# Output projection and FFN one slot later, in the order Q, O, V, F, K, in a fused linear-attention and FFN kernel

## The reference, cut to what matters

```python
q, k, v = x @ Wq.T + bq, x @ Wk.T + bk, x @ Wv.T + bv      # each cut into 16 heads of 32
q, k = exp(q), exp(k)
kv  = cumsum(k[:, :, :, None] * v[:, :, None, :], axis=1)  # running sums over the 2048 rows
k1  = cumsum(k, axis=1)
num = einsum('zsD,zsDd->zsd', q, kv)
den = sum(q * k1, axis=-1, keepdims=True)
x1  = layernorm(x + (num / den as 512 columns) @ Wo.T + bo)
h   = x1 @ weight @ aux_weight1 @ aux_weight2
out = layernorm(x1 + tanh(h + bias))
```

## Time and profile before

| | |
|---|---|
| median of 3 runs | 2304.31 us (2303.34 to 2304.90) |
| the profiled execution | 2303.22 us, of which the span of its records is 2301.4 us |
| granted clock of PE over the span | 0.993 |
| busy share of the span | PE 97%, PE weight loads 80%, DVE 70%, POOL 56%, ACT 44% |
| DMA | 243.17 MB moved, 106 GB/s on average |

### The profile page before, as it was taken

How to read it: one execution, slowest core, us unless ns; L and a number is a source line. 1 busy time by engine, 2 the same in 40 slices (tenths; PEclk the granted TensorE clock), 3 DMA queues, 4 the chain that set the end, 5 groups by cost and what they waited for, 6 DMA issues and landing times.

```text
span 2301.4 us, 77308 instructions
## 1 busy us (share of the span) xinstructions
PE 2241.9 (97%) x27752; PEld 1829.6 (80%) x27752; DVE 1617.2 (70%) x2456; ACT 1012.3 (44%) x1695; POOL 1294.2 (56%) x1797
## 2 busy tenths in 40 slices
PE   7999999999999999999999999999999999999985
PEld 6778888888888888888888888888888888887864
DVE  5576776776776776776776776776776776767674
ACT  4344444444444444444444444444444444444432
POOL 1356556556556556556556555555555555555554
PEclk9999999999999999999999999999999999999997
DMA  7133333333333333333333333333333333333221
GB/s 183 57 110 111 104 111 111 103 111 112 103 110 112 103 111 111 102 111 112 102 109 114 103 110 112 103 111 111 104 112 109 105 108 112 106 103 108 71 70 56
DMA packets 294574, 243.17 MB, mean 106 GB/s; under 512 B 33424, under 2 KB 225936, under 8 KB 294288
## 3 DMA queue, kind: packets, MB, share of 16 engines
q1 hardware_dynamic: 293136, 236.59, 33.3%
q10 hardware_dynamic: 1152, 2.10, 0.3%
HBM read 139.99 MB, written 98.57 MB: 104 GB/s over the span
## 4 chain that ended last, share of the span: by engine, by line
PE 95%; DVE 2%; issue 1%; SPq 1%; ACT 1%; DMA 1%; POOL 0%; POOLq 0%; DVEq 0%; ACTq 0%
PE SC L326 26%; PE SC L328 25%; PE SC L327 25%; PE SC L417 6%; PE ND L393 5%; PE ND L384 3%; PE ND L380 2%; PE ND L428 2%; DVE o L803 1%; DMA WK<-wT 0%; SPq L253 0%; ACT A L648 0%; DVE WK L816 0%; SPq L241 0%; PE ND L327 0%
## 5 line engine op out<-in xcount | busy, mean ns | idle before, releaser
L916 POOL TENSOR_SCALAR_AFFINE_SELECT A<-A 128x512 f32<-128x512 f32 x512 | 331.8, 682 | 321.1 <-ACT A L648 321.0
L803 DVE RECIPROCAL o<-ND 128x512 f32<-128x512 f32 x128 | 427.8, 3342 | 0.1
L857 DVE TENSOR_TENSOR xres<-SC,xres 128x512 f32<-128x512 f32 x128 | 88.5, 692 | 431.8 <-PE SC L328 431.6
L910 POOL TENSOR_TENSOR oL<-o,oH 128x512 fp32r<-128x512 f32 x128 | 166.4, 1300 | 327.0 <-ACT oH L627 327.0
L638 ACT ACTIVATE WK<-xres,shift,rstd 128x512 f32<-128x512 f32 x128 | 104.1, 814 | 531.7 <-POOL shift L951 531.7
L648 ACT ACTIVATE A<-SC 128x512 f32<-128x512 f32 x512 | 264.7, 603 | 43.3 <-PE SC L417 43.3
L326 PE MATMUL SC<-xTH,WqH 128*128 128x512 f32 x512 | 210.8, 412 | 9.5 <-ACT QT L598 3.7
L326 PE MATMUL SC<-WfH,x1H 128*128 128x512 f32 x512 | 201.0, 393 | 14.4 <-issue 7.9
L816 DVE TENSOR_TENSOR_SCAN WK<-ones,k,KT 128x128 f32<-128x128 f32 x512 | 207.5, 467 | 7.1 <-PE ND L380 6.8
L326 PE MATMUL SC<-WoH,oH 128*128 128x512 f32 x512 | 201.1, 393 | 11.3 <-issue 9.3
L598 ACT ACTIVATE QT<-SC,bcol 128x512 f32<-128x512 f32 x128 | 88.4, 690 | 270.4 <-PE SC L328 270.4
(11 more groups left out here) (103 smaller groups left out, 4983.3 us busy)
## 6 DMA issues: line engine op xcount, KB each, us to landing
xres<-x SPq DMA_DIRECT2D x128, 256.0 KB, 2.6
x_rows<-WK SPq DMA_DIRECT2D x128, 256.0 KB, 3.1
WK<-x_rows SPq DMA_DIRECT2D x512, 64.0 KB, 2.0
out<-WK SPq DMA_DIRECT2D x128, 256.0 KB, 2.0
xin<-x SPq DMA_DIRECT2D x504, 64.0 KB, 1.9
k_rows<-WK SPq DMA_DIRECT2D x120, 256.0 KB, 2.0
WK<-k_rows SPq DMA_DIRECT2D x480, 64.0 KB, 2.2
A<-a1T ACTq DMA_DIRECT2D x4, 256.0 KB, 5.4
```

Of the source, the lines that this page charges most:

```text
L803: nc.vector.reciprocal(o[:, :, :], den_ps).then_inc(recip_ready, 1)
L857: nc.vector.tensor_tensor(r, oproj_ps, r, ALU.add).then_inc(r_ready, 1)
L910: nc.gpsimd.tensor_tensor(oL[:, :, :], o[:, :, :], oH[:, :, :].bitcast(F32), ALU.subtract).then_inc(ol_ready, 1)
L916: last = nc.gpsimd.affine_select(out=A[:, k % 2, j, :, :], in_=A[:, k % 2, j, :, :], compare_op=ALU.is_ge, fill=0.0, base=0, pattern=[[0, ...
```

## The change

The tail of O and F moves by one slot: in slot k, O is that of tile k-2 and F that of tile k-3; the program has one more slot at its end (`run_slots(..., 4)`). PE's slot is now `first_half` (small, Q, O, V) and `second_half` (F, K), and K is the last product ahead of the next slot's scores. The other engines' slots are written in a new order to match. DVE turns x1s of tile k-3 ahead of the reciprocal of tile k-1, and z is the last instruction of its slot. ACT makes x1 after the copy of V and takes K's exponential late; POOL makes `x1L` ahead of `oL`; SP stores and loads K, loads x, and only then stores x1 and loads it back.

The block loads are written in another form: each of the four transfers fills all 128 partitions with one piece, and on the DRAM side it is 4 groups by 32 rows by one piece (`x_b`, `k_blocks`, `x1_blocks`, `load_blocks`). At the start of the program the loads of the two auxiliary weights go from ACT's queue to SP's, between those of x, and the loads of Wq and Wk go from SP's queue to ACT's; the splitting of the FFN weight (`split_w`) stands behind the first exponential of K.

```diff
-    x_b = x.rearrange("b (i t p) (a f) -> b i a p t f", t=P // HD, p=HD, a=HG)
+    x_b = x.rearrange("b (i t p) (a f) -> b i t a p f", t=P // HD, p=HD, a=HG)
...
-    k_blocks = k_rows.rearrange("(a p) (t c) -> t p a c", a=HG, t=HG)
-    x1_blocks = x1_rows.rearrange("(t p) (a f) -> a p t f", t=HG, a=HG)
+    k_blocks = k_rows.rearrange("(a p) (t c) -> a t p c", a=HG, t=HG)
+    x1_blocks = x1_rows.rearrange("(t p) (a f) -> t a p f", t=HG, a=HG)
...
+        def load_blocks(engine, tile, a, semaphore):
+
+            rows = a.rearrange("(a f p) n -> f a p n", a=HG, p=HD)
+            for f in range(NK):
+                engine.dma_start(tile[:, f, :], rows[f]).then_inc(semaphore, 16)
...
-            def load_by_block(tile, a, semaphore):
-                rows = a.rearrange("(a f p) n -> a p f n", a=HG, p=HD)
-                for j in range(HG):
-                    sp.dma_start(tile[j * HD:(j + 1) * HD], rows[j]).then_inc(semaphore, 16)
...
             def load_x(c, n):
-                for j in range(HG):
-                    sp.dma_start(x_buffer(c, n)[j * HD:(j + 1) * HD, :].rearrange("p (t f) -> p t f", t=HG),
-                                 x_b[n % B, c.it + n // B, j]).then_inc(xin_loaded[n % B], 16)
+                for t in range(HG):
+                    sp.dma_start(x_buffer(c, n)[:, t * P:(t + 1) * P],
+                                 x_b[n % B, c.it + n // B, t]).then_inc(xin_loaded[n % B], 16)
...
+                    for a in range(HG):
+                        sp.dma_start(Ktok[:, a * P:(a + 1) * P], k_blocks[a]).then_inc(ktok_loaded[n % B], 16)
...
                     wait_before(sp, (x1_stored[n % B], c.dma_count(n)), (x1l_ready, c.count(n)))
-                    for j in range(HG):
-                        sp.dma_start(x1s[j * HD:(j + 1) * HD, :].rearrange("p (t f) -> p t f", t=HG),
-                                     x1_blocks[j]).then_inc(x1s_loaded[n % B], 16)
...
+                    for t in range(HG):
+                        sp.dma_start(x1s[:, t * P:(t + 1) * P], x1_blocks[t]).then_inc(x1s_loaded[n % B], 16)
...
             first = Chunk(0)
+            load_aux(0)
             load_x(first, 0)
+            load_aux(1)
             load_x(first, 1)
-            load_by_block(wq_raw, wqT, wq_loaded)
+            load_aux(2)
             load_x(first, 2)
+            load_aux(3)
             load_x(first, 3)
-            load_by_block(wk_raw, wkT, wk_loaded)
             load_biases()
...
-                    wait(pe, z_ready, c.count(k - 2))
+                    wait(pe, z_ready, c.count(k - 3))
                     wait(pe, k_ready, c.count(k + 4))
                     wait(pe, v_ready, c.count(k))
-                    wait(pe, r_ready, c.count(k - 1))
+                    wait(pe, r_ready, c.count(k - 2))
...
+            def first_half(c, k):
+                small(c, k)
+                if c.exists(k + 4):
+                    queries(c, k)
+                    if c.exists(k - 2):
+                        output_projection(c, k)
+                if c.exists(k):
+                    values(c, k)
+                    if not c.exists(k + 1):
+                        denominators(c, k)
+                        attend(c, k)
+
+            def second_half(c, k):
+                if c.exists(k - 2) and not c.exists(k + 4):
+                    output_projection(c, k)
+                if c.exists(k - 3):
+                    feed_forward(c, k)
+                if c.exists(k + 4):
+                    keys(c, k)
...
             split_aux(0)
+            load_blocks(act, wq_raw, wqT, wq_loaded)
             split_aux(1)
+            load_blocks(act, wk_raw, wkT, wk_loaded)
...
             split_wq_wk(0)
             split_wq_wk(1)
-            split_w()
             split_a12()
...
-            keep_q(*ahead(-4))
-            split_x(*ahead(-4))
-            keep_k(*ahead(-4))
+            keep_q(*place(-4))
+            split_x(*place(-4))
+            keep_k(*place(-4))
+            split_w()
...
+                if c.exists(k - 3):
+                    n = k - 3
+                    wait(dve, x1s_loaded[n % B], c.part_count(n))
+                    nc.vector.transpose(x1s[:, :], x1s[:, :]).then_inc(x1_turned, 1)
+                if att and c.exists(k - 1):
                     normalise(k - 1)
```

More of the change, by code:

```diff
@@ L217, in updates_state, with place @@
                 return not self.static() or 0 <= B * self.it + n < NT - B
-        def ahead(tile):
+        def place(tile):
             return Chunk(tile // B), tile % B
@@ new lines, in _, with align, keys @@
+            f_place, k_place = 0, 48
+            def align(c, place):
+                if not c.static():
+                    pe.addr_align(256, offset=place, max_nops=255)
+            def keys(c, k):
+                align(c, k_place)
+                b, ns, att = k % QUAD, 1 - (k // QUAD) % 2, c.exists(k)
+                if not att:
+                    pe.wait_ge(wkh_ready, b + 1)
+                    pe.wait_ge(wkl_ready, b + 1)
+                if att:
+                    wait(pe, scores_out[1], c.count(k + 1))
+                wait(pe, k_ready, c.count(k + 4))
+                three_pass(kproj_ps, lambda f: WkH[:, f, b * P:(b + 1) * P],
+                           lambda f: WkL[:, f, b * P:(b + 1) * P], lambda f: xTH[:, ns, f, :],
+                           lambda f: xTL[:, ns, f, :], None if c.static() else k_place).then_inc(kproj_done, 1)
@@ L521, in _ @@
             multiply_aux()
-            queries_and_keys(*ahead(-4))
-            queries_and_keys(*ahead(-3))
+            queries(*place(-4))
+            keys(*place(-4))
+            queries(*place(-3))
+            keys(*place(-3))
             multiply_weight()
-            queries_and_keys(*ahead(-2))
-            queries_and_keys(*ahead(-1))
+            queries(*place(-2))
+            keys(*place(-2))
+            queries(*place(-1))
+            keys(*place(-1))
             multiply_bv()
@@ L538, in _ @@
                 for k in range(B):
[L539 to L547 removed]
+                    second_half(c, k)
+                    first_half(c, k + 1)
+            second_half(*place(NT - 2 * B))
+            for t in range(NT - 2 * B + 1, NT + 3):
+                first_half(*place(t))
+                second_half(*place(t))
         @block.scalar
@@ L672, in slot, with copy_v @@
                                          scale=rstd[:, 1:2]).then_inc(out_ready, 1)
-                if att and not c.exists(k + 1):
-                    split_o(k)
-            def aux_rows(a, f):
-                return a.rearrange("(k p) n -> k p n", p=P)[f]
-            for f in range(NK):
-                act.dma_start(a1T_raw[:, f, :], aux_rows(a1T, f)).then_inc(aux_loaded[f], 16)
-                act.dma_start(a2_raw[:, f, :], aux_rows(a2, f)).then_inc(aux_loaded[f], 16)
+            def copy_v(c, k):
+                wait(act, v_done, c.count(k + 1))
+                wait(act, state_done, c.state_count(k - 1))
+                nc.scalar.activation(V[:, k % 2, :], v_ps, ACT.Copy).then_inc(v_ready, 1)
             split_aux(0)
+            load_blocks(act, wq_raw, wqT, wq_loaded)
             split_aux(1)
-            split_x(*ahead(-8))
+            load_blocks(act, wk_raw, wkT, wk_loaded)
+            split_x(*place(-8))
             split_aux(2)
-            split_x(*ahead(-7))
+            split_x(*place(-7))
             split_aux(3)
-            split_x(*ahead(-6))
-            split_x(*ahead(-5))
+            split_x(*place(-6))
+            split_x(*place(-5))
             split_wq_wk(0)
             split_wq_wk(1)
-            split_w()
             split_a12()
@@ L846, in slot @@
+                if att and c.exists(k - 1):
+                    normalise(k - 1)
+                if att and not c.exists(k + 1):
+                    normalise(k)
                 if c.exists(k - 2):
                     n = k - 2
-                    wait(dve, x1s_loaded[n % B], c.part_count(n))
-                    nc.vector.transpose(x1s[:, :], x1s[:, :]).then_inc(x1_turned, 1)
-                if att and not c.exists(k + 1):
-                    normalise(k)
-                if prev:
-                    wait(dve, xres_loaded[(k - 1) % B], c.dma_count(k - 1))
+                    wait(dve, xres_loaded[n % B], c.dma_count(n))
@@ L863, in _ @@
+                if c.exists(k - 3):
+                    n = k - 3
+                    wait(dve, ffn_done, c.count(n + 1))
+                    wait(dve, out_stored[(n - 2) % B], c.dma_count(n - 2))
+                    nc.vector.tensor_tensor(y[:, n % 2, :], ffn_ps, bfbc[:, :], ALU.add).then_inc(z_ready, 1)
             first = Chunk(0)
@@ L886, in _ @@
             add_bo()
-            run_slots(dve, slot, 3)
+            run_slots(dve, slot, 4)
         @block.gpsimd
```

366 lines of the change are left out of this document (155 added, 211 removed).

## The result

The changed kernel takes 2395.6 us (2390.8 to 2399.0) against 2304.5: 1.0395 times as long, with a 95% interval of 1.0376 to 1.0413, or +91 us. The forecast was slower, +62.5, 2367 us in a range of 2299 to 2460.

A forecast was written before the change was run, and what follows sets the result against it. The prediction took PE's own stream to bound the loop. Its terms, 18.5 - 3 + 20 + 11 + 8 + 8 = +62.5 us, on a median of 2304.3 gave 2367 us, in a range of 2299 to 2460.

The forecast's parts named there:

- the forecast's own case: Whole kernel: four engines carry the block loads and the slot just fits; 2367 us, chance 0.42, own range 2345 to 2395.
- Four engines or 16: Block loads: whether their new form confines each transfer to four DMA engines, as forecast, or leaves it on all 16.
- The start, +20: Up to slot 3: loads on four engines bring slot 0's Q at 97 us, not 68.39; +20 net of smaller gains.
- K's wait, +18.5: Ahead of the scores: K's exponential, first in the list of waits, comes late; 0.15 us a slot, 121 slots, +18.5.
- The circle, +11: In the loop: turn of x1s, reciprocal, x1, store, loads, next turn; 16.8 to 17.3 us against 17.4, just fitting, +11.
- The rival in which the circle becomes the slot's bound: In the loop: the four engines, or the circle through them, set the slot; +67 instead of 11, 2423 us, chance 0.30.
- The loop's exit, -3: Where the loop is left: one slot more of slack for O and F covers the late input to PE; -3 us.
- Last slots and drain, +8 and +8: After slot 124: one more round of O, x1 and F, less waits for oL, +8; five rounds 1.7 longer each, +8.
- The rival of 16 engines: Whole kernel: all 16 engines carry the loads, K's wait is paid, the start gains 14; 2314 us, chance 0.17.
- the gain of 5.6 from the late split: At the start: splitting the FFN weight later removes PE's idle 3.74; with auxiliary weights and Wq from two queues, 5.6.

The follow-up runs named there:

- e1: The changed kernel with all block loads (x, x1s, Ktok, four weights) written wide, as before the change: 2331.1 us, 1.0112 times before.
- e2: The kernel before with nothing but its block loads in the changed, narrow form: 2344.3 us, 1.017 times before.
- e5: e1 with the scores' wait for K's exponential moved from first to last in their list, which has one entry fewer: 2315.5 us, 1.0052 times before.
- e6: e1 with the products of F and K exchanged, so that F is last again: 2314.0 us, 1.0047 times before.
- e8: The kernel before with the scores reordered and the wait for F's sum put on the first matmul into bank 0: 2309.8 us, 1.0024 times before.
- e3: The changed kernel, narrow loads kept, with the turn of x1s put behind the reciprocal and multiplication on DVE: 2369.0 us, 1.0274 times before.
- e4: The changed kernel with only the x1s loads in the wide form of before: 2364.4 us, 1.0255 times before.
- e9: The changed kernel with e1, e3 and e6 combined, the start's load order of before, and O ahead of F in the drain: 2296.0 us, 0.9967 times before.
- e7: The changed kernel with the diffs of e1 and e3 together: wide loads and the late turn of x1s: 2325.1 us, 1.0087 times before.
- e10: The kernel before with only the split of the FFN weight moved behind the first exponentials of Q and K: 2301.0 us, 0.9986 times before.

## Why the prediction was right or wrong

The direction, the cause and the range held; the size was 62.5 where 91 came (95.9 between the two profiled spans), and 2395.6 lies just above the 2345 to 2395 that I gave the forecast's own case. Term by term:

- *Four engines or 16.* Right, by the count of completion packets and by e1 and e2. By the Trainium skill ("DMA: Bandwidth & Descriptors", "Why a DMA increments its semaphore by 16 and not by 1") the number of engines is the largest one up to 16 that divides the slowest dimension of both sides, which is four for 128 and 4. The trace agrees: 12 completion packets fewer for each of 1520 transfers. The "plain division" in my words had no row behind it.
- *The start, +20.* Measured +24.2, with Q of slot 0 at 100.9 for my 97, and from there to slot 3 8.3 less than before for my 8.4. The 97 was in part luck, since two errors nearly cancel. The last tile of x has landed by 82.22 and not at 94; four engines, at 99 GB/s between 20 and 30 us, are faster than the 77 that I took from an average. And from there it is 18.7 us to Q of slot 0 and not 3, because the splitting of two weights on ACT and the fourth Q and K still stand between. I had counted the bytes on the four engines and not what waits behind them: SP's issuing, and the quarter of the auxiliary weights that lies on these four.
- *K's wait, +18.5.* Right in size: 0.15 a slot forecast (121 slots at 0.15 are 18.2, the 18.5 is a slip), and 18.2 in 109 slots with wide loads (e1), or 0.167. e5 and e6 show that it is the place in the list, as put. One step was wrong without showing: I had read that PE already waited for z before. e8 shows that den and num covered z's wait but for 0.01 a slot. So the price is what goes beyond that cover: den to scores is 1.16 where den and num alone take 1.00.
- *The circle, +11.* Measured 9.7 (after against e1). The circle was put at 16.8 to 17.3 and came to 17.3 and 17.4; wide it is 14.8 and 15.2, put at 14.9. What I had not named is how it reaches PE: x1 stands ahead of K's exponential on ACT, so a late x1 delays the scores of the next slot. The rival in which the circle becomes the slot's bound holds in part: 43 of 109 slots are longer for it, but it costs 9.7 in the loop and not 67. That the four engines are full is not the reason, by e3 and e4.
- *The loop's exit, -3.* Wrong in sign: 112 to 124 is 7.1 longer, 1.9 of it K's wait. The slot of slack did take the old stall away, as e5, e6 and e9 show (-3). But with a circle as long as the slot there was no slack to spend: the 4.04 on DVE went through x1 and K's exponential to PE. In e3 and e4, with a shorter circle, this stretch is only 2.1 and 0.4 us longer than in e1.
- *Last slots and drain, +8 and +8.* This is the step that failed: +36.7. Narrow loads cost 18.1 there and not 8 (after against e1): 2.2 to 2.5 in each of five rounds instead of 1.7, and the first turn behind slot 124's den comes 4.9 later on top of that. The circle sets slots 125 to 127 too, with 19.2, 17.3 and 17.4 from turn to turn. The turn ahead of the reciprocal costs 10.2 (e1 against e7), not 4, since it acts in three rounds and not in one: turn to turn 14.8, 15.2 and 28.1 in e1, 13.2, 13.7 and 22.0 in e7. The tile more is left with 8.3 (e7 against before), and there I had 3.6: F to F is 11.6 and 11.0 in e7, as put, but the first of these three F comes 32.2 behind den of slot 127, where the first of before's two came 26.8.
- *The rival of 16 engines* was put at 2314 and e1 came to 2331. Two steps of it failed, the drain as above, and the start: the gain of 5.6 from the late split is real (e10, 4.5), but in the changed kernel the aux weights lie between the tiles of x, the first Q starts at 29.84 instead of 23.00, and nothing of it is left before slot 0. With the loads of the start in the order of before (e9) slot 3 comes at 98.2.

Not settled: why DVE stands still for up to 4 us after the loop is left, why e7's start is 3.2 us longer than e1's, and why e6's executions lie up to 5.5 us apart.

## What to carry to other kernels

The size of a transfer's outermost dimension is worth checking first: four groups instead of 32 rows cost 64 us here, and the sign of it is in the page, in the count of packets under 512 bytes. When steps are moved by a slot to give slack, add up the circle that the new order closes, stores and loads included, and ask what stands behind its members on each engine; a circle as long as the slot gives no slack to anything. And where the last product changes, let its wait be the last in the list: with one entry dropped on the way, that was 15.6 us here.

## What the runs showed of the hardware

- A transfer with 4 groups outermost in DRAM and 128 partitions in SBUF ran on four engines. They moved 99 GB/s between 20 and 30 us, 25 each, where 16 engines together moved 251, 16 each, in the same stretch of e1.
- Issuing stood still while four engines were behind: four issues of 64 KB took 12.55 us of SP where they took 1.96 with wide loads (e1), and what SP had to issue next waited with them. On ACT three issues of Wk took 10.79, and ACT computed nothing for 10.64.
- A transfer over 16 engines lands as late as its part on the slowest: 24 of the 32 parts of one pair of auxiliary weights had landed by 17.94, the eight on the four busy engines by 27.67.
- The semaphore instructions ahead of the scores begin 0.11 us apart, so a late wait is paid with all that stand behind it: 0.36 us from K's exponential to the scores with its wait in the first of three, 0.20 at most in the second of two (e5). As long as den and num ran longer than that, 1.00, next to nothing of it was to be seen.
